# Group norm, shifted blocks and Hadamard mix of 16 images: four quarters of four batches as a pipeline in place of whole-batch stages

## The reference

```python
x = x + _L0_conv_ref(_gn(x), L0_conv_offset)   # shift each channel by its offset, then a 3x3 Gaussian
x = x + _L1_conv_ref(_gn(x))                    # 384 channels times a 512 x 512 Hadamard matrix, cut to 384
```

## Time and profile before

| what | value |
|---|---|
| median of 3 runs | 356.97 us (355.29 to 358.61) |
| profiled execution: span from first to last instruction | 361.2 us |
| busy: DVE, PE, ACT, POOL | 246.9, 162.4, 159.2, 124.9 us |
| bytes moved, mean rate over the span | 76.67 MB, 212 GB/s |
| mean granted PE clock | 0.818 |

### The profile page before, as it was taken

The page is one execution under the profiler, slowest core; times in us unless marked ns, Lnnn a source line. Parts: engine busy times, 40 slices in busy tenths (PEclk is TensorE's granted clock), DMA queues, the critical chain, the costliest instruction groups (busy, mean ns, idle before and its releaser), DMA issues.

```text
span 361.2 us, 3084 instructions
## 1 busy us (share of the span) xinstructions
PE 162.4 (45%) x804; PEld 98.4 (27%) x804; DVE 246.9 (68%) x322; ACT 159.2 (44%) x205; POOL 124.9 (35%) x62
## 2 busy tenths in 40 slices
PE   0000004682796890300000008677676776767782
PEld 0000003682796790300000003222222222222230
DVE  1999999771874764100000047999999999899995
ACT  1029994940311200100000078787777777687720
POOL 0000000000521112000000007797979797979750
PEclk9999999995698996555555558698989889898898
DMA  6999999994388974373373300724996566874449
GB/s 227 414 410 409 409 370 355 406 249 102 71 216 216 279 210 122 53 87 44 44 87 44 44 0 17 292 100 186 356 373 248 191 147 198 311 294 181 190 181 360
DMA packets 21545, 76.67 MB, mean 212 GB/s; under 512 B 3824, under 2 KB 3952, under 8 KB 21376
## 3 DMA queue, kind: packets, MB, share of 16 engines
q1 hardware_dynamic: 18992, 69.62, 57.0%
q0 software_dynamic: 1616, 4.78, 4.8%
q10 hardware_dynamic: 912, 2.02, 4.7%
HBM read 46.42 MB, written 29.99 MB: 212 GB/s over the span
## 4 chain that ended last, share of the span: by engine, by line
DMA 25%; DVE 18%; issue 18%; another core or an unknown queue 16%; SPq 9%; ACTq 5%; ACT 5%; PE 2%; DVEq 0%; POOLq 0%
DMA ring<-x_pad 19%; DVE ring L917 9%; DVE parts L260 6%; SPq L267 5%; ACTq L267 5%; ACT blk L513 3%; DMA ring<-x_rows 2%; DMA blk<-x_pad 2%; DMA stat_rows<-blk_stat 2%; ACT parts L546 1%; SPq L271 1%; PE ps L656 1%; DVE blk_half L845 1%; PE ps L573 1%
## 5 line engine op out<-in xcount | busy, mean ns | idle before, releaser
L656 PE MATMUL ps<-parts,had_sb 128*128 128x512 f16 x384 | 101.6, 426 | 101.9 <-DVE parts L260 98.3
L513 ACT ACTIVATE blk<-ring,gn 128x1024 f32<-128x1024 f32 x48 | 58.6, 1230 | 85.4 <-DMA ring<-x_rows 59.9
L656 PEld LDWEIGHTS ps<-parts,had_sb 128*128 128x128 f16 x384 | 39.5, 107 | 163.7 <-DVE parts L260 105.2
L260 DVE TENSOR_TENSOR parts<-blk,parts 128x1024 f16<-128x1024 f32 x33 | 64.1, 1948 | 2.5 <-ACT parts L546 2.5
L917 DVE SCALAR_TENSOR_TENSOR ring<-ps,ring 128x1024 f32<-128x1024 f32 x48 | 57.2, 1210 | 0.0
L249 POOL TENSOR_TENSOR other_a<-blk 128x1024 f32<-128x1024 f32 x8 | 24.2, 3025 | 90.8 <-ACT parts L546 73.4
L253 POOL TENSOR_TENSOR blk<-blk 128x1024 f32<-128x1024 f32 x15 | 48.4, 3224 | 1.2
L582 PE MATMUL ps<-geo_sb,blk 128*128 128x128 f32 x72 | 13.6, 357 | 69.6 <-DMA blk<-x_pad 56.3
L595 PE MATMUL ps<-parts 128*128 128x64 f32 (+4 forms) x306 | 41.3, 301 | 7.3 <-ACT parts L475 6.2
L546 ACT ACTIVATE parts<-blk 128x1024 f16<-128x1024 f32 x40 | 41.2, 1048 | 4.2 <-POOL blk L253 2.8
L595 PEld LDWEIGHTS ps<-parts 128*128 128x128 f32 x306 | 40.7, 216 | 8.1 <-ACT parts L475 6.6
(11 more groups left out here) (105 smaller groups left out, 116.0 us busy)
## 6 DMA issues: line engine op xcount, KB each, us to landing
ring<-x_pad SPq DMA_DIRECT2D x20, 1536.0 KB, 15.3
out<-ring SPq DMA_DIRECT2D x13, 1536.0 KB, 6.3
blk<-x_pad SPq DMA_DIRECT2D x18, 512.0 KB, 8.3
x_rows<-blk POOLq DMA_DIRECT2D x9, 512.0 KB, 4.3
out<-ring SPq DMA_DIRECT2D x9, 512.0 KB, 3.7
ring<-x_rows ACTq DMA_DIRECT2D x5, 384.0 KB
ring<-x_rows SPq DMA_DIRECT2D x4, 384.0 KB
ring<-x_rows SPq DMA_DIRECT2D x9, 128.0 KB
```

The lines of the kernel that those rows point to most:

```text
L260: eng.tensor_tensor(parts[:, n % 2, 1, s, :], source, parts[:, n % 2, 0, s, :], ALU.subtract).then_inc(low_done[s], 1)
L513: act.activation(target, ring[:, t, place_of(i), :], ACT.Identity, bias=gn[:, t, i % BATCH, 1:2], scale=gn[:, t, i % BATCH, 0:1]).then_inc ...
L656: last = pe.matmul(sums[:, h, :], had_sb[:, sign, :], parts[:, n % 2, part, s, 512 * h:512 * (h + 1)], start=(at == 0 and part == 0), stop ...
```

## The change

The batches are cut into four quarters of four. Each quarter goes through norm, blocks, gather and Hadamard stage; while the products of quarter w run, norm and blocks of w+1 and the statistics of w+2 are mixed in between them by a written order on every engine (w is called a window below). In particular:

- **Blocks**: a slot of a quarter is 8 channels x 4 batches = 32 partitions. Four slots make a unit of 128 partitions; a quarter has three units, of 4, 4 and 1 slots. Transposes and masks are done for a unit at once. The convolution writes each slot's sums to its own 32 partitions of PSUM, with 32 columns of weights.
- **Norm of a unit**: its numbers come from small matmuls with selection matrices (`to_unit`, `to_group`), not through DRAM; `gn_rows` and `stat_rows` are gone.
- **Patches** become gathers: six indirect transfers a quarter from POOL, each for one tile and two batches, each partition taking its own row, partitions of unchanged channels being out of bounds.
- **Hadamard stage**: no normalised copies and no sums a+c, a-c. Tile a is multiplied in float32 by H scaled with its norm (`w_a`, made by POOL); b and c go in as float16 high and low parts that carry the scale. One PSUM pair per batch collects a - b + c, is read by DVE, gets 2b added, is read, gets -2c added, and is read again. The norm's mean comes in as a bias that is computed once a quarter.
- **Rests** (`low`): DVE makes them for the first batch of a quarter (one instruction each), POOL for the other three (two instructions each).
- **Statistics** of quarters 1 to 3: DVE has five tiles a quarter, ACT seven. The ring has 10 places; nothing is reloaded.
- The offsets are ranked with three small matmuls on 48 partitions in place of 48x48 comparisons.

```diff
+QUARTERS, QUARTER = 4, 4
+RING = 10
+FAST, UNITS, PER_UNIT = 9, 3, 4
+ORDER = (1, 0, 2)
+def dve_tiles(i):
+    return (0, 1) if i < QUARTER or i % QUARTER == 3 else (0,)
...
         def _(pool):
+            def gather_rows(q, slots):
+                for k in range(2):
+                    first_place = place_of(QUARTER * q + 2 * k)
+                    for t in range(CT):
+                        pool.indirect_dma_start(
+                            ring[:, t, first_place:first_place + 2, :].rearrange("p b n -> p (b n)"), None,
+                            x1_rows[q][0:BIND * slots, :].rearrange("r (k n) -> (r k) n", k=2), bass.IndirectOffsetOnAxis(index[:, t, k:k + 1], 0),
+                            bounds_check=2 * BIND * slots - 1, oob_is_err=False).then_inc(gathered[t][k], 16)
...
+                pool.tensor_scalar(scaled[:, :], ring[:, 1 + s, place_of(n), :], scale[:, q % 2, 1 + s, b:b + 1], None, ALU.mult).then_inc(scaled_done, 1)
+                pool.wait_ge(scaled_done, lows[0])
+                pool.wait_ge(high_done[s], n + 1)
+                pool.tensor_tensor(parts[:, n % 2, 1, s, :], scaled[:, :], parts[:, n % 2, 0, s, :], ALU.subtract)\
+                    .then_inc(pool_low, 1)
...
         def _(pe):
+            def convolve_strips(slots):
+                for bank in range(2):
+                    for j in range(3 * bank, 3 * bank + 5):
+                        lo = max(4 * j - 1, 16 * bank)
+                        hi = min(4 * j + 5, 16 * bank + 16)
+                        for s, k in enumerate(slots):
+                            last = pe.matmul(summed[32 * s:32 * s + 32, bank, 32 * (lo - 16 * bank):32 * (hi - 16 * bank)],
+                                             flip[:, j, 32 * s:32 * s + 32], conv_w[:, k, lo - (4 * j - 1):hi - (4 * j - 1), :],
+                                             start=(j == 3 * bank), stop=(j == 3 * bank + 4), skip_group_check=True)
...
+                if j == 1:
+                    if units:
+                        transposes(g)
+                    add_b(n)
+                    product_a(n + 1)
+                    if units:
+                        convolve(g)
+                    add_c(n)
+                    if units:
+                        transposes(g + 1)
+                    products_bc(n + 1)
...
         def _(dve):
+            for n in range(BATCH):
+                w, j = n // QUARTER, n % QUARTER
...
+                if j == 1:
+                    result(n, 1)
+                    if units:
+                        mask(g)
+                    result(n, 0)
+                    result(n, 2)
+                    if units:
+                        add(g)
+                        mask(g + 1)
```

More of the change, by code:

```diff
@@ new lines, in _ @@
+            for i in range(QUARTER):
+                load(i)
+            sp.wait_ge(place_done, 1)
+            at = [(sp.value_load(place[0:1, k, 0:1], min_val=PIXELS, max_val=PIXELS + SLOT * (OFFSETS - 1)),
+                   sp.value_load(place[0:1, k, 1:2], min_val=1, max_val=2 * PIXELS + SLOT * (OFFSETS - 1) - 1))
+                  for k in range(FAST)]
+            fetch(0)
+            for i in range(QUARTER, RING):
+                sp.wait_ge(load_in[place_of(i - 4)], 16)
+                load(i)
@@ new lines, in gather, with weights @@
+            def gather(q):
+                for u in range(UNITS):
+                    pool.wait_ge(x1_out[u], 16 * (q + 1))
+                with pool.If(active > FAST):
+                    pool.wait_ge(more_out, 16 * MORE * (q + 1))
+                    gather_rows(q, OFFSETS)
+                with pool.If(active < FAST + 1):
+                    gather_rows(q, FAST)
+            def weights(n):
+                q, b = n // QUARTER, n % QUARTER
+                pool.wait_ge(scale_ready, q + 1)
+                if n >= 4:
+                    pool.wait_ge(product_done, CT * (n - 4) + 1)
+                pool.tensor_scalar(w_a[:, n % 4, :], geo_of("h"), scale[:, q % 2, 0, b:b + 1], None, ALU.mult).then_inc(weights_ready, 1)
@@ new lines, in root_second, with high @@
+            def root_second(q):
+                act.wait_ge(var2_ready, q + 1)
+                act.activation(root2[:, :, :], var2[:, :, :], ACT.Sqrt, bias=column("eps2"), scale=2.0).then_inc(root2_done, 1)
+            def high(n, s):
+                q, b = n // QUARTER, n % QUARTER
+                act.wait_ge(scale_ready, q + 1)
+                act.wait_ge(gathered[1 + s][b // 2], 16 * (q + 1))
+                if n >= 2:
+                    act.wait_ge(product_done, CT * (n - 2) + 2 + s)
+                act.activation(parts[:, n % 2, 0, s, :], ring[:, 1 + s, place_of(n), :], ACT.Copy,
+                               scale=scale[:, q % 2, 1 + s, b:b + 1]).then_inc(high_done[s], 1)
@@ new lines, in product @@
+            def product(n, s, sign, stop):
+                for part in range(2):
+                    if part == 0:
+                        pe.wait_ge(high_done[s], n + 1)
+                    elif by_vector(n, s):
+                        pe.wait_ge(vector_low, lows_before(n, s, True) + 1)
+                    else:
+                        pe.wait_ge(pool_low, lows_before(n, s, False) + 1)
+                    for h in range(2):
+                        last = pe.matmul(ps[n % 2][:, h, :], had_sb[:, 128 * sign:128 * (sign + 1)], parts[:, n % 2, part, s, 512 * h:512 * (h + 1)],
+                                         start=False, stop=stop and part == 1, skip_group_check=True)
+                return last
@@ new lines, in _ @@
+            last.then_inc(ranked, 1)
+            pe.wait_ge(geo_in, 16)
+            pe.wait_ge(had_in, 16)
+            pe.wait_ge(index_done, 1)
+            active = pe.value_load(count_i[0:1, 0:1], min_val=0, max_val=OFFSETS)
+            sum_means(0)
+            sum_about(0)
+            pe.wait_ge(conv_w_done, 1)
+            for u in range(UNITS):
+                transposes(u)
+                convolve(u)
+            more_blocks(0)
+            sum_second(0)
+            sum_bias(0)
@@ new lines, in _ @@
+            link(mean_and_variance(QUARTER - 1, stats_at[QUARTER - 1]))
+            means(0)
+            spread_means(0)
+            keep_moments(0)
+            unit_moments(0)
+            unit_scales(0)
+            for u in range(UNITS):
+                mask(u)
+                stats_at[QUARTER + u] = take_stats(QUARTER + u)
+                add(u)
+                mean_and_variance(QUARTER + u, stats_at[QUARTER + u])
+            all_moments(0)
+            second_shift(0)
+            second_scale(0)
```

1537 lines of the change are left out of this document (863 added, 674 removed).

## The result

The changed kernel took **337.54 us** (334.19 to 340.89), the kernel before 356.36 (355.29 to 358.61) on the same chip: ratio 0.943, 95% interval 0.934 to 0.952. The profiled execution has a span of 334.7 us; the forecast's own sum was 338.7 for the span and 334 for the median. Times are medians of all executions, with the lowest and the highest in brackets, while a ratio that has an interval compares the means of those executions alone that lie within 1.5% of their kernel's fastest.

The account below looks back on a forecast made before the run. No single engine but the chain of waits was taken as the bound. Start 93, windows 68.7, 64.1, 57.2 and 28.7, end 5, surcharges 9 and 13 gave a span of 338.7, taken as 334 us median; range 316 to 352.

Parts of the forecast that it names:

- surcharges: Added to the summed steps: 9 us for POOL's rests slowing DVE, 13 us for PE's clock below full.
- Convolution: Blocks on PE: 80 records for a four-slot unit taken at 5.5 us, a one-slot unit at 2.5.
- rival 1: Convolution strips run one after another: four-slot unit 9.4 or 15.9 us, total 365 or 423, middle 390; chance 0.18.
- Clock: PE steps on the path in windows: granted clock 0.89 taken from the earlier Hadamard stage, adding 13 us.
- Second sums: PE's 32 records per quarter for the next quarter's norm, at j = 3 in windows with units: 3.8 us.
- product_a: PE's float32 product of tile a in each batch: four times a float16 pass, 1.7 us.
- POOL beside DVE: POOL's rests slow DVE's small chains in the windows: 3 us a window, 9 in all.
- no slack: First half of a quarter's gathers, three issues, has 12 us and needs about 12.
- Rival 2: Gathers land late, at the patches' 56 GB/s: 6 us a quarter, 24 in all, total 358; chance 0.12.
- Start and end: Time to the first result, 93 us, and the last store with the end, 5 us.
- DMA never at full share after the first 30 us: Sign expected in the changed kernel's profile: DMA engines not at full share once 30 us have passed.
- some 65 come back as waits: Of some 90 us idle latency in norms and patches, mostly gone, some 65 return as waits inside the windows.

Follow-up runs that it names:

- a1: Changed kernel with the convolution's two inner loops exchanged, so that one slot's strip follows another in each bank: 378.5 us, ratio 1.065.
- a4: Changed kernel with all 32 float16 rests made by DVE, none by POOL: 337.9 us, ratio 0.953.
- a5: Changed kernel with two POOL operations of 2.8 us each put ahead of each quarter's gathers: 348.17 us, ratio 0.978.
- a2: Changed kernel with the second sums moved earlier on PE, the units' part ahead of the last batch's add_b: 324.96 us, ratio 0.904.
- b1: Kernel before with only its patches replaced by 12 indirect transfers from POOL, stages kept: 311.25 us, ratio 0.868.
- a9: a2 with SP's block fetches for the quarter after next held until the next quarter's gathers have landed: 313.33 us, ratio 0.866.
- c1: a9 timed again, side by side with a repeat of b1 on one chip: 319.26 us, 0.894 by medians.
- a10: Changed kernel with only the later block fetch of a9, second sums left in place: 339.35 us, ratio 0.934.

## Why the prediction was right, and what was wrong inside it

**The sum, piece by piece**, surcharges put where they were meant. Forecast: start 93, windows 75.1, 70.5, 63.6, 31.5, end 5. Measured: 88.0, 76.0, 73.2, 61.9, 32.5, 3.1. Together 338.7 and 334.7. No piece is off by more than 5 us, but several terms are, and they cancel. That idle latency would go and return in part as waits is what the runs show; that the sum came within 4 us is in part luck:
- *Convolution*: the 720 matmuls take 37.9 us, where 8 units of 5.5 and 4 of 2.5 make 54. Mis-sized, 16 too high. It was priced near 4.0 and raised for the number of records; 80 records cost 2.72, less than the 34 of one block in the earlier trace rows. At the 1.88 us that four records of product_a, 1024 columns, take at full clock, the 5888 columns one after another would be an estimated 10.8 us. a1 shows that rival 1 was the right danger: in turn they cost 7.3 to 9.5. The Trainium skill's rule for 32-column tiles (TensorEngine Tiling (Array Packing), Theoretical Speedup), up to four times, agrees in kind; measured is 2.7 times.
- *Clock*: mis-sized, too low. I took the 0.89 of the Hadamard stage; the windows had 0.75 to 0.79. PE's work there comes in bursts: before the stretch from 95.0 to 102.6, which was granted 0.50, it had been idle for 5.39 us. Not every pause does this: one of 2.57 us stood before the unit at 126.10, granted 0.61, and an equal one before the unit at 198.95, granted 1.00, which took 2.72 us. Second sums took 28.4 us in four (L701 and L706), not 15; product_a 45.4 in sixteen, not 27; first sums 12.4, not 7. That is 37 more against a surcharge of 13; some 3 of it are product_a's price, 1.88 at full clock where I had 1.7.
- *POOL beside DVE*: forecast 9, a4 shows 11.4 in four groups of small DVE instructions. Right in place, and in size as far as busy time goes. But POOL was forecast 110 us busy and had 163. Its rests took 121.1 of them (L470 and L473), since the operation with one tensor input takes 2.88, where I went by the 1.9 of another; the other 42 are what the forecast left out, above all 24.2 of indirect issues, 11.2 of scaled weights `w_a` and 7.0 of block stores.
- *Gathers*: "no slack" was about 3 us too strict (a5). Rival 2 is out here, and comes back as soon as the second sums are moved (a2). The transfers land in 6.9 us at the median, beside 56 us for the patches. Six issues at 1.0 us and 0.3 between them hold POOL for 7.6 us a quarter; the forecast had no row for this price. The Trainium skill's rule on ports (SBUF — State Buffer, Door 1: The DMA port swizzle) goes that way; b1 shows the gain, not that ports are its cause.
- *Start and end*: 5 and 2 too high.
- *Signs*: "DMA never at full share after the first 30 us" was wrong. The share was 1.02 from 30 to 60 us and 1.00 from 215 to 225, and a2 shows what such a stretch costs the gathers once the sums are early.
- *Slips in the working*: the steps of a batch of window 3 add up to 7.3 us, not 7.4. The parts of the chances are 0.51 for my forecast and 0.13 for late gathers, where 0.52 and 0.12 stand. Neither moves the forecast.

**Where the expected gain went.** A window with products alone takes 32.5 us. Norm and blocks make it 61.9, 29.4 more, and statistics 11 to 14 more again. So the change spends 88.0 + 3 x 29.4 + (76.0 + 73.2 - 2 x 61.9) = 201.6 us on all that is not products, and four times 32.5 on products. b1 reaches its first product at 163.35, with the same norm and blocks in stages. Its products then take 145 us, where the change spends 133 with the last store, so what the change loses is lost in the start and the interleaving and not in its new form of the product. The interleaved steps are hardly hidden. PE and DVE hand one PSUM pair back and forth, and against window 3, window 2 has 29.8 us more of PE's work and 18.8 more of DVE's, and is 29.4 longer: about as much as PE's part alone. a1 shows the same, where PE's 39.6 us more cost 41. DVE's work finds some gaps: in a4, 14 us more of it cost 1.2. That each step of PE stands in the line with its full length is argued from these sums; only the convolution and the second sums were tried by themselves. The prediction named this ("some 65 come back as waits"), and took the rest of the gain for the pipeline's. b1 shows that it is the gathers': they alone bring some 47 us (ratio 0.868), and all the rest of the change, the pipeline above all, gives some 27 back (0.943). a2 and a9 win much of that again, by taking one wait of 8 us a quarter away and then clearing the way of what was late next.

What stays open: why the same kernel came out at 0.894 in c1 and at 0.866 in a9, on the same chip (0.880 and 0.857 when counted as the intervals are). The kernel before took 357.3 us beside c1 and 361.8 beside a9, which is a little over one point of the ratio; the profiled executions had nearly the same waits (24.0 and 22.6 us for the gathers) and granted clocks of 0.837 and 0.851. Nor is it shown whether the patches were slow because of the partitions that they reach. Nor was it tried whether two PSUM pairs for the results would make the interleaved steps free.

## What to carry to other kernels

Before a pipeline is built to fill a stage in which nothing computes, mend the transfers of that stage: here 12 indirect transfers did more than the whole pipeline. A step put between two engines that hand one buffer back and forth is hardly hidden: here window 2 grew by as much as PE's added work. So count such a step as path, at the clock granted in its own stage (0.75 to 0.79 here), and not as cover. When a wait is taken away, look in the new trace for the next late one, and for who shares its resource: early sums alone gave 4 points of the ratio, and moving the block fetches behind the gathers gave 2 to 5 more (0.904 to 0.857 in a9 and 0.880 in c1), where without the early sums it gave nothing (a10).

## What the runs showed of the hardware

- A GpSimd operation with one tensor input and a scalar per partition (128x1024, float32) takes 2.88 us at the mean in the changed kernel (shortest 2.83); with two tensor inputs 2.17 (shortest 2.12).
- A DVE instruction of 128x3 elements (L1005) takes 0.16 us without POOL's rests and 1.12 at the mean of four with them, up to 2.07.
- Four 32-column strips in turn cost 2.7 times what they cost interleaved, for the same 80 matmuls (7.32 and 2.72 us, both at a granted clock of 1.00).
- An indirect transfer costs GpSimd 1.0 us to issue and 0.3 until the next, with two batches each and, in b1, with four. The mean of 1.23 in b1 comes from the three that are issued within the Hadamard stage, at 1.91; the nine before it take 1.0.
